# Expert tiles of a two-layer transformer block: biases by matmul, the second ReLU on VectorE, and a new order of steps

## What is computed

```python
# layer 0: 128 -> 512 -> 128, for each of 8 experts, kept for the tokens that chose it
h = jax.nn.relu(flat_x @ W1[e] + b1[e])
y = h @ W2[e] + b2[e]
# layer 1: 128 -> 256 -> 256 -> 128
h1 = jax.nn.relu(jnp.einsum('bsh,ehm->bsem', x, W1) + b1)
h2 = jax.nn.relu(jnp.einsum('bsem,emn->bsen', h1, W2) + b2)
out_e = jnp.einsum('bsen,enh->bseh', h2, W3) + b3
```

## Time and profile before

| | us |
|---|---|
| median of 3 runs | 754.67 |
| lowest and highest | 746.63 and 755.76 |
| the profiled execution | 749.76 |
| its span on the core | 747.9 |

### The profile page before, as it was taken

One profiled execution on the slowest core, in us unless ns is written; L12 is line 12 of the kernel. 1 busy time (PEld: TensorE's weight loads), 2 busy tenths in 40 slices (PEclk: granted clock), 3 DMA queues, 4 the chain that ended last, 5 costly groups with the idle time before them and its releaser, 6 DMA issues.

```text
span 747.9 us, 10481 instructions
## 1 busy us (share of the span) xinstructions
PE 494.3 (66%) x3533; PEld 387.7 (52%) x3533; DVE 400.3 (54%) x819; ACT 299.6 (40%) x837; POOL 249.9 (33%) x212
## 2 busy tenths in 40 slices
PE   2675857768588975467777677766777737766522
PEld 2464536556477864156666666544665526543311
DVE  1679989693866476500000100697626647856743
ACT  0243434434356653023323355332666634325421
POOL 1718573424813545530000400546230242425100
PEclk9787779976799998555555799786999959955555
DMA  9700000000244341134344567101345210000000
GB/s 323 213 16 0 1 1 1 1 1 15 65 133 117 104 128 29 49 96 108 108 118 126 156 190 194 31 1 47 107 123 140 65 36 4 1 1 4 1 4 7
DMA packets 79011, 53.54 MB, mean 72 GB/s; under 512 B 14608, under 2 KB 72912, under 8 KB 78704
## 3 DMA queue, kind: packets, MB, share of 16 engines
q1 hardware_dynamic: 76432, 48.37, 22.9%
q0 software_dynamic: 2048, 4.20, 1.9%
q10 hardware_dynamic: 480, 0.32, 0.2%
HBM read 44.34 MB, written 8.52 MB: 71 GB/s over the span
## 4 chain that ended last, share of the span: by engine, by line
PE 36%; DVE 29%; ACT 12%; issue 12%; POOL 4%; another core or an unknown queue 2%; DMA 1%; SPq 1%; DVEq 0%; POOLq 0%; ACTq 0%
PE PS L711 6%; PE PS L720 5%; DVE cond_ptbd L1131 3%; PE PS L694 3%; ACT hid L787 3%; DVE rot_qk L1312 3%; DVE rot_qk L1320 3%; POOL cond_kbd L981 2%; ACT hid L781 2%; PE PS L687 2%; DVE rot_ptbd L1340 2%; DVE rot_sh L1309 2%; DVE arena L1508 2%; PE PS L1207 2%
## 5 line engine op out<-in xcount | busy, mean ns | idle before, releaser
L1170 POOL TENSOR_TENSOR rot_sh<-rot_sh,const 128x1024 f32<-128x1024 f32 x16 | 49.3, 3091 | 55.2 <-DVE rot_sh L1309 55.2
L640 POOL DMA_INDIRECT picked<-slots_y,place_u x32 | 31.9, 995 | 104.7 <-DMA slots_y<-slot_y 96.3
L981 POOL TENSOR_TENSOR cond_kbd<-cond_qkv,const 128x2048 f32<-128x2048 f32 x16 | 58.5, 3654 | 21.3 <-ACT cond_qkv L1068 21.3
L720 PE MATMUL PS<-expert_w,hid 128*128 128x128 f32 x360 | 63.1, 321 | 2.6 <-ACT hid L787 2.0
L934 DVE SCALAR_TENSOR_TENSOR acc<-picked,weight,acc 128x128 f32<-128x128 f32 x8 | 2.8, 349 | 110.4 <-DMA picked<-slots_y,place_u 108.7
L711 PE MATMUL PS<-hid,expert_w 128*128 128x128 f32 x240 | 49.0, 368 | 19.4 <-ACT hid L781 19.3
L787 ACT ACTIVATE hid<-PS,expert_b 128x128 f32<-128x128 f32 x120 | 37.6, 365 | 48.4 <-PE PS L711 42.9
L720 PEld LDWEIGHTS PS<-expert_w,hid 128*128 128x128 f32 x360 | 54.7, 227 | 4.1 <-ACT hid L781 3.0
L711 PEld LDWEIGHTS PS<-hid,expert_w 128*128 128x128 f32 x240 | 42.2, 265 | 27.1 <-issue 26.9
L694 PE MATMUL PS<-slot_xT,expert_w 128*128 128x128 f32 x240 | 47.8, 334 | 2.4 <-ACT slot_xT L776 1.4
L781 ACT ACTIVATE hid<-PS,expert_b 128x128 f32<-128x128 f32 x120 | 37.6, 365 | 23.1 <-PE PS L694 20.9
(11 more groups left out here) (265 smaller groups left out, 1172.6 us busy)
## 6 DMA issues: line engine op xcount, KB each, us to landing
expert_w<-in_moe_w_dram SPq DMA_DIRECT2D x90, 256.0 KB, 3.0
expert_w<-in_moe_w_dram SPq DMA_DIRECT2D x60, 128.0 KB, 2.6
slot_x<-slots_x SPq DMA_DIRECT2D x60, 64.0 KB
slots_y<-slot_y SPq DMA_DIRECT2D x60, 64.0 KB, 2.3
slots_x<-zeros SPq DMA_DIRECT2D x2, 960.0 KB, 6.4
wqk<-in_attn_qk_dram SPq DMA_DIRECT2D x1, 1024.0 KB, 8.3
arena<-in_attn_qk_dram SPq DMA_DIRECT2D x1, 1024.0 KB, 8.8
expert_b<-in_moe_b_dram SPq DMA_DIRECT2D x60, 2.0 KB, 2.6
```

The costliest lines, as they stand in the source:

```text
L640: nc.gpsimd.indirect_dma_start(picked[:, j, n, :], None, ys[half], bass.IndirectOffsetOnAxis(place_u[job % 2][:, j, n:n + 1], 0)).then_inc ...
L720: mm = nc.tensor.matmul(full(MB_[i % 2], 0, E), hid[:, i % 2, c, :], W[i % WB][:, lo + E * (c - first):lo + E * (c - first) + E], start=(c ...
L981: nc.gpsimd.tensor_tensor(ckbd[:], cqkv[s][:, P:2 * P].unsqueeze(1).to_broadcast([P, CH, P]), k["headmask"].unsqueeze(2).to_broadcast([P, ...
L1170: nc.gpsimd.tensor_tensor(here, here, k["sin"].unsqueeze(1).to_broadcast([P, NC_ * SEQ, S]), ALU.mult).then_inc(rotated[part], 1)
```

## The change

The biases of the hidden layers no longer come in through the ReLU. Each bias is split into three bf16 parts that add up to it, in the first block, by POOL (six casts and four subtractions on 8 partitions x 512), and kept in DRAM. For each tile SP loads the three parts (3 x 512, bf16) and PE adds them with one matmul for each 128 inner columns (`add_bias`, four more bf16 matmuls a tile) ahead of the matmuls proper. relu_a becomes one ACT instruction of 256 columns; relu_b becomes one DVE instruction of 256 columns. All tiles now use bank 1 for T and a (`MA_`) and bank 7 for b and out (`MB_`). The whole table `TIMES` is new, so the order changes in all parts of the program. Two feed-forward tiles move to other memory.

```diff
 TIMES = {
-    "m_relu_b": (143.8, 147.8, 151.8, 155.4, 159, 163.7, ...
+    "m_relu_b": (156.9, 161.7, 166.7, 170.7, 173.4, 178.2, ...
...
-        MB_ = (1, 7)
+        MA_, MB_ = (1,) * 4, (7,) * 4
...
-        WBIAS = [sb(f"expert_b{n}", [P, FF0 // P]) for n in range(WB)]
+        WBIAS = [sb(f"expert_b{n}", [3, FF0], BF16) for n in range(WB)]
...
+                for l in range(2):
+                    sp.dma_start(bias_in[l], d[f"moe{l}_b"].rearrange("e p c -> e (p c)")).then_inc(loaded["bias_in"], 16)
                 for n in range(2):
                     sp.dma_start(ffn_w[n][:], d[f"ffn_w{n}"]).then_inc(loaded["ffn"], 16)
...
+                pool.wait_ge(loaded["bias_in"], 16 * 2)
+                own_split = Own()
+                for l in range(2):
+                    left = bias_in[l].rearrange("e (p c) -> e c p", c=FF0 // P)
+                    for part in range(3):
+                        nc.gpsimd.tensor_copy(bias_parts[l][:, part], left).then_inc(bias_split, 1)
+                        pool.wait_ge(bias_split, own_split.next())
+                        if part < 2:
+                            nc.gpsimd.tensor_tensor(bias_left, left, bias_parts[l][:, part], ALU.subtract).then_inc(bias_split, 1)
+                            pool.wait_ge(bias_split, own_split.next())
+                            left = bias_left
...
-                claim(pe, (MB_[i % 2],), (m_y_ready, i + 1))
-                nc.tensor.transpose(full(MB_[i % 2], 3 * P, 4 * P), slot_x[i % XB][:], k["ident"]).then_inc(m_xT_ps, 1)
+                if i >= 2:
+                    pe.wait_ge(m_b_ps, i - 1)
+                claim(pe, (MA_[job_of(i)[0]],), (m_xT_ready, i + 1))
+                nc.tensor.transpose(full(MA_[job_of(i)[0]], 3 * P, 4 * P), slot_x[i % XB][:], k["ident"]).then_inc(m_xT_ps, 1)
+
+            def add_bias(i, bank, at, f):
+                nc.tensor.matmul(full(bank, at, at + P), WBIAS[i % WB][:, P * f:P * f + P], ones_b[0:3, :], start=True, stop=False)
...
             def relu_a(i):
                 act.wait_ge(m_a_ps, i + 1)
-                for c in range(2):
-                    ins = nc.scalar.activation(hid[:, i % 2, c, :], full(MB_[i % 2], P * c, P * c + P), ACT.Relu, bias=WBIAS[i % WB][:, c:c + 1])
-                ins.then_inc(m_a_ready, 1)
+                if i >= 2:
+                    act.wait_ge(m_out_ps, i - 1)
+                nc.scalar.activation(hid[:, i % 2, 0:2, :].rearrange("p c t -> p (c t)"), full(MA_[job_of(i)[0]], 0, 2 * P), ACT.Relu).then_inc(m_a_ready, 1)
...
+            def relu_b(i):
+                dve.wait_ge(m_b_ps, i + 1)
+                if i >= 2:
+                    dve.wait_ge(m_out_ps, i - 1)
+                nc.vector.tensor_scalar(hid[:, i % 2, 2:4, :].rearrange("p c t -> p (c t)"), full(MB_[job_of(i)[0]], 0, 2 * P), 0.0, None, ALU.max).then_inc(m_b_ready, 1)
```

More of the change, by code:

```diff
@@ L126 @@
[L126 to L130, removed]
@@ L290 @@
+    "f_finish": (432.5, 458.5, 485.2, 527.5, 555.6, 577, 593.1, 609.3),
 }
@@ L425, in build @@
         zeros = sb("zeros", [P, E])
-        loaded = {n: sem(f"loaded_{n}") for n in ("x", "const", "cond_w0", "small", "attn", "blank", "bias", "cond_w1", "ffn", "level", "log")}
-        blanked = sem("blanked")
+        bias_in = [picked[0:EXPERTS, l].rearrange("e n f -> e (n f)") for l in range(2)]
+        bias_left = xT_half[0:EXPERTS, :].rearrange("e (c p) -> e c p", p=P)
+        bias_parts = [t.rearrange("e (s c p) -> e s c p", s=3, p=P) for t in (uT[0:EXPERTS, 0:3 * FF0 // 2].bitcast(BF16), acc[0:EXPERTS].rearrange("e n f -> e (n f)")[:, 0:3 * FF0 // 2].bitcast(BF16))]
+        bias_dram = [nc.dram_tensor(f"bias_parts{l}", (EXPERTS, 3, FF0), BF16, kind="Internal").ap() for l in range(2)]
+        loaded = {n: sem(f"loaded_{n}") for n in ("x", "const", "cond_w0", "small", "attn", "blank", "bias", "cond_w1", "ffn", "level", "log", "bias_in")}
+        blanked, bias_split, bias_kept = sem("blanked"), sem("bias_split"), sem("bias_kept")
         prep = sem("prep_step")
@@ L692, in hidden_a @@
                 pe.wait_ge(w_loaded[i % WB], weights_up_to(i))
+                claim(pe, (MA_[job],), (m_a_ready, i + 1))
                 for f in range(2):
-                    mm = nc.tensor.matmul(full(MB_[i % 2], P * f, P * f + P), W[i % WB][:, P * f:P * f + P], slot_xT[i % 2][:], start=True, stop=True)
+                    add_bias(i, MA_[job], P * f, f)
+                    mm = nc.tensor.matmul(full(MA_[job], P * f, P * f + P), W[i % WB][:, P * f:P * f + P], slot_xT[i % 2][:], start=False, stop=True)
                 mm.then_inc(m_a_ps, 1)
@@ L717, in slots_out @@
                 pe.wait_ge(m_b_ready, i + 1)
+                claim(pe, (MB_[job],), (m_y_ready, i + 1))
                 first, lo = ((0, FF0), (2, 3 * FF1))[layer]
                 for c in range(first, 4):
-                    mm = nc.tensor.matmul(full(MB_[i % 2], 0, E), hid[:, i % 2, c, :], W[i % WB][:, lo + E * (c - first):lo + E * (c - first) + E], start=(c == first), stop=(c == 3))
+                    mm = nc.tensor.matmul(full(MB_[job], 2 * P, 3 * P), hid[:, i % 2, c, :], W[i % WB][:, lo + E * (c - first):lo + E * (c - first) + E], start=(c == first), stop=(c == 3))
                 mm.then_inc(m_out_ps, 1)
@@ L775, in copy_slots @@
                 act.wait_ge(m_xT_ps, i + 1)
[L776 removed]
+                nc.scalar.activation(slot_xT[i % 2][:], full(MA_[job_of(i)[0]], 3 * P, 4 * P), ACT.Copy).then_inc(m_xT_ready, 1)
             def relu_a(i):
                 act.wait_ge(m_a_ps, i + 1)
[L780 to L788 removed]
+                if i >= 2:
+                    act.wait_ge(m_out_ps, i - 1)
+                nc.scalar.activation(hid[:, i % 2, 0:2, :].rearrange("p c t -> p (c t)"), full(MA_[job_of(i)[0]], 0, 2 * P), ACT.Relu).then_inc(m_a_ready, 1)
             def copy_out(i):
@@ L793, in copy_out @@
                     act.wait_ge(m_stored[i % YB], 16 * (i // YB))
-                nc.scalar.activation(slot_y[i % YB][:], full(MB_[i % 2], 0, E), ACT.Copy).then_inc(m_y_ready, 1)
+                nc.scalar.activation(slot_y[i % YB][:], full(MB_[job_of(i)[0]], 2 * P, 3 * P), ACT.Copy).then_inc(m_y_ready, 1)
             def copy_x(half):
@@ L877, in places @@
                 width = HT * EXPERTS
+                if job >= 2:
+                    dve.wait_ge(m_done, HT * (job - 1))
                 dve.wait_ge(counting, 2 * job + 1)
@@ L1697, in _ @@
             def _(sp):
+                for l in range(2):
+                    sp.dma_start(bias_dram[l], (uT[0:EXPERTS, 0:3 * FF0 // 2], acc[0:EXPERTS].rearrange("e n f -> e (n f)")[:, 0:3 * FF0 // 2])[l].bitcast(BF16).rearrange("e (s f) -> e s f", s=3)).then_inc(bias_kept, 16)
                 sp.wait_ge(blanked, 1)
```

295 lines of the change are left out of this document (149 added, 146 removed), and 80 rows, old and new, of the table TIMES.

## The result

The changed kernel takes 834.35 us (median of 4 runs, 830.28 to 841.51) against 752.95 for the kernel before: ratio 1.110, 95% interval 1.100 to 1.121. It is 11% slower, where I forecast 722, 4% faster. The profiled execution has a span of 833.8.

The account below looks back on a forecast made before the run. Bound: PE and ACT taking turns in job 1, PE at 1.2 GHz. 749.8 + 3 (first block) + 6 (job 0) - 32.5 (job 1) - 4.5 (job 2) = 721.8, so 722 us; range 702 to 746.

Parts of the forecast that it names:

- the price of the bias matmuls: Jobs 1 and 2, PE: four bf16 matmuls cost 0.39 us, so the biases add 0.4 us a tile.
- The clock: Job 1: PE works a whole tile or more without a gap over 0.2 us, so its clock rises from 1.2 GHz.
- The rival that job 1 stays at 1.2 GHz: Job 1 at 4.65 us a tile saves 14 us, nothing in job 2, total 745 us; chance 0.14.
- The rival that ended slower: Jobs 0 and 3: relu_b stands behind DVE attention instructions, PE waits; 2 us a tile, +60, total 776; chance 0.06.
- Job 1: Feed-forward tiles running alone: new order hides ReLU waits and the clock rises; 55 us against 87.6, -32.5 us.
- Job 2: Second feed-forward job running alone: begins at full clock, its first three tiles save 1.5 us each, -4.5 us.
- First block: Start of the kernel: ten added POOL operations end the block between 22.3 and 27 us; +3, bounds +0.3 to +5.5.
- the front parts lose more: Rival: first block at +5.5 and job 0 at +24 us, total 742 us; chance 0.08.
- Job 0 and relu_b: Job 0, shared with attention: 15 relu_b instructions move to DVE at 0.42 us each, +6 us.
- Job 3: Last job, shared with attention: ACT loses 13 us, DVE gains 6, neither full; 0, bounds -8 and +10 us.

Follow-up runs that it names:

- e11: The changed kernel with the three bias rows padded with zeros to 128 rows, same result: 713.69 us, ratio 0.963 to the kernel before.
- e13: e11 with the order (table of numbers) of the kernel before: 746.87 us, ratio 0.995 to the kernel before.
- e9: The changed kernel with two bias matmuls a tile in place of four, half of the biases missing: 724.48 us, ratio 0.974.
- e3: The changed kernel without bias matmuls and split, biases added in two-instruction ReLUs, with the order of the kernel before: 769.0 us, ratio 1.022.
- e1: The changed kernel with only the order (whole table of numbers) of the kernel before put back: 859.5 us, ratio 1.143.
- e14: e11 with relu_b on ScalarE, one instruction of 256 columns: 711.22 us, ratio 0.959 to the kernel before.

## Why the prediction was wrong, point by point

**The step that failed is the price of the bias matmuls.** I wrote "Four bf16 matmuls took 0.39 us, so the biases cost 0.4 a tile". The row says `128*128 128x128`, the new instruction is `3*128 3x128`, and it stands between f32 matmuls of 128 rows. I matched type and columns and not rows. With 128 rows the price is the one that I took (0.11 each, 0.44 a tile, in e11); with 3 rows it is 0.35 to 0.36 each at full clock, 1.4 us a tile, and 0.50 each at 1.2 GHz, 2.0 a tile. The sum took the 0.4 as a fixed number, without an upper bound.

**The clock.** I expected it to rise since PE would work "a whole tile or more without a gap longer than 0.2". In after, the tiles of job 2 show no gap, PE is busy 83 of 86.8 us, and the clock stays at 0.50. In e13 it has gaps of 0.68 and 0.50 in each tile and the clock is 0.94. So the gaps in PE's rows are a poor sign. What after has and e11 has not is matmuls that don't follow at their usual distance, and it has twice as many of them as e9: the earlier trace rows had records at 0.22 us ahead of the rise, while in after two records of a and b take 0.73. That this distance is what keeps the clock down is an inference from these runs; e3, with neither bias matmuls nor a rise in job 1, shows that it is not the only thing that does. The rival that job 1 stays at 1.2 GHz was the right one in kind, but at 4.65 us a tile, and I gave it job 1 alone. Measured were 6.0 to 6.4 us a tile in both jobs. The rival that ended slower had another mechanism (DVE ahead of relu_b), which did not come in after: 3.9 us of waits in all, not 60. It came in part with the old order: 15.6 and 9.3 us in jobs 0 and 3 of e13.

**Job 1, without the bad price.** Forecast 55 us with 3.0 for the tiles in the new order; e11 has 54.6, with tiles from 3.0 on. But I had put all of the 32.5 us down to the order, and e13, with the old order, has 29.1 of them. The size was right, the cause was not: the order is not what brings the greater part. **Job 2**: forecast -4.5; e11 has 41.6 to the last T where before had 53.1, -11.5, since besides the cold start the stall of the earlier trace rows is gone.

**First block.** Forecast +3, between 22.3 and 27; measured 25.05 - 22.07 = 2.98. (My upper end of +5.5 should have been +4.9, 27 less 22.07.) **What lies before job 0** also lost 9 us more (196.8 to 208.6, of which 3 are the block). I had no term for it: e1 and e13, with the old order, begin job 0 at 198.2 and 200.5, so it belongs to the new order of attention steps. My rival "the front parts lose more" meant the first block and job 0.

**Job 0 and relu_b.** Forecast +6 with 0.42 each. The duration is right: 0.425 at most, in all 60. By the Trainium skill, "GPSIMD Engine Reference", section "Specifications", POOL contends with DVE instructions that have two SBUF inputs or use a 2-port mode. The trace agrees: relu_b has one input, from PSUM, and no instance is longer than the others. But its time lies beside other work: e11's stretch from job 0 to job 1 is 117.8 against 120.0, and e14 shows no gain from ScalarE. **Job 3**: forecast 0; from its first T to the end 227.3 before (71.9 + 155.4) and 226.7 in e11. The 0 is two changes that cancel: job 3 itself is 15.6 us shorter in e11, what follows it 15.0 longer. PE had stood 6.4 and 6.0 us for relu_a and relu_b in job 3 before, and the new order hides nearly all of that.

Put together, e11 at a ratio of 0.963 is 28 us under the kernel before, which is the gain that I had summed up (749.8 to 722), with job 2 better and the part before job 0 worse than I said. That the sums agree is in part luck: jobs 0 to 3 and the part before job 0 moved by other amounts than my terms, or for other reasons, and the differences cancel. One price decided the sign.

## What to carry to other kernels

When a small matmul is put among large ones, look at its row count before its type or its columns: pad the contraction with zero rows to 128 if its neighbours have 128, since the padded matmul cost 0.11 us at full clock and 0.21 at 1.2 GHz, and the 3-row one 0.35 and 0.50. Read PE by the distance between starts of like records, not by its busy share: in job 2 of after PE was busy 96% of the stretch, and a third of each tile went to four matmuls of 3 rows. And a price that the trace of before does not show needs an upper end in the sum, worked out to the point where the sign turns: a forecast gain of 33 us over 240 new matmuls is 0.14 us each, so a price of 0.24 in place of 0.10 would have turned it, if every one of them lies on PE's path. And test the cause of a gain apart from its size: here the clock rose with the old order too.

## What the hardware showed unexpectedly

- A matmul of 3 or of 64 rows between matmuls of 128 rows costs two interruptions: with two f32 records behind it 0.94 us at 1.2 GHz and 0.58 at 2.4, padded to 128 rows 0.64 and 0.33.
- A bf16 matmul of 128 rows among f32 ones costs 0.11 us at 2.4 GHz: 0.05 to the records behind it, and those two take 0.28 (399.65 to 399.93) in place of 0.22.
- PE stayed at 1.2 GHz for 180 us (jobs 1 and 2 of after) while its rows were busy 168 of them.
- The first 120 bias matmuls of 3 rows cost 0.012 of before's time, hardly more than the noise, the next 120 cost 0.136. What goes with it is whether the clock rises.
- Open: with biases in the ReLUs and the old order (e3) a tile of job 1 stayed at 5.8 us, with the padded bias matmuls and the same order (e13) the clock rose. The runs do not part whether the shorter ReLUs or PE's added work does that.
